# Three graph attention layers over 16 batches: one transpose-and-add moved from TensorE to VectorE blocks and adding transfers

## The reference

```python
def gat(inp, mask, W, a):                      # one attention layer
    h = inp @ W
    e = leaky_relu((h @ a1)[:, :, None] + (h @ a2)[:, None, :], 0.2)
    e = where(mask > 0, e, -9e15)              # layers 2 and 3 only
    return elu(softmax(e, axis=2) @ h)

h = relu(layernorm(x))
out = relu(h @ mlp1_w + mlp1_b)                # 128 -> 256; o1 below
out = elu(gat(out, None, W_fc, a_fc)) + out    # layer 1, 256 wide; z below
out = relu(out @ mlp2_w + mlp2_b)              # 256 -> 128; o2 below
out = elu(gat(out, adj, W_hand, a_hand)) + out # layer 2, 128 wide
x = x + relu(out)
h = relu(layernorm(x))
return x + elu(softmax(masked e) @ (h @ W))    # layer 3, 128 wide
```

## Time and profile before

| | |
|---|---|
| median of three runs | 432.31 us (431.66 to 434.0) |
| span of the profiled execution, first to last instruction | 429.0 us |
| lowest run less that span | 2.7 us |
| median run less that span | 3.3 us |
| granted TensorE clock, mean | 0.994 |
| TensorE busy | 411.1 us (96%) |
| VectorE busy | 357.8 us (83%) |
| ScalarE busy | 315.7 us (74%) |
| GpSimd busy | 24.9 us (6%) |
| DMA traffic | 36.42 MB, mean 85 GB/s |

### The profile page before, as it was taken

One profiled execution on the slowest core, in us unless ns is written; L12 is line 12 of the kernel. 1 busy time (PEld: TensorE's weight loads), 2 busy tenths in 40 slices (PEclk: granted clock), 3 DMA queues, 4 the chain that ended last, 5 costly groups with the idle time before them and its releaser, 6 DMA issues.

```text
span 429.0 us, 8704 instructions
## 1 busy us (share of the span) xinstructions
PE 411.1 (96%) x2544; PEld 352.7 (82%) x2544; DVE 357.8 (83%) x1226; ACT 315.7 (74%) x764; POOL 24.9 (6%) x53
## 2 busy tenths in 40 slices
PE   6999999999999999999999999999999999989782
PEld 4688779887898899797998788989879799869772
DVE  7786588878998898988898868979698899889974
ACT  2655659658796787786878688687867887799774
POOL 0000000000001000010100000100000000000000
PEclk9999999999999999999999999999999999999997
DMA  7854323123423142232222213222320122120001
GB/s 209 278 146 130 105 74 121 74 76 98 125 98 75 53 138 84 52 101 74 75 82 68 75 53 98 79 72 74 80 87 10 49 93 59 45 80 24 27 1 57
DMA packets 39461, 36.42 MB, mean 85 GB/s; under 512 B 4080, under 2 KB 30320, under 8 KB 39408
## 3 DMA queue, kind: packets, MB, share of 16 engines
q1 hardware_dynamic: 37408, 33.17, 26.1%
q10 hardware_dynamic: 2000, 2.63, 1.8%
HBM read 31.46 MB, written 4.32 MB: 83 GB/s over the span
## 4 chain that ended last, share of the span: by engine, by line
PE 87%; DVE 5%; ACT 3%; issue 2%; DMA 1%; SPq 0%; POOL 0%; ACTq 0%; DVEq 0%
PE bank L1530 24%; PE bank L1437 23%; PE bank L1426 13%; PE bank L1416 6%; PE bank L1477 6%; PE bank L1455 6%; PE bank L1445 3%; PE bank L1538 2%; PE bank L1496 1%; PE bank L1466 1%; DMA row<-row_scratch 1%; DVE stats L1036 1%; DVE u L1265 1%; ACT ext L826 1%; ACT e L911 1%
## 5 line engine op out<-in xcount | busy, mean ns | idle before, releaser
L1530 PEld LDWEIGHTS bank<-ext,prob 128*128 128x128 f32 x1024 | 119.6, 192 | 6.3 <-issue 4.9
L1530 PE MATMUL bank<-ext,prob 128*128 128x129 f32 x1024 | 122.1, 275 | 0.3 <-DVE prob L1207 0.2
L1437 PE MATMUL bank<-ext,prob 128*128 128x257 f32 x512 | 119.0, 380 | 0.0
L1437 PEld LDWEIGHTS bank<-ext,prob 128*128 128x128 f32 x512 | 94.8, 190 | 17.3 <-issue 4.5
L1211 DVE SCALAR_TENSOR_TENSOR prob<-prob,square,mask_t 128x512 f32<-128x512 f32 x98 | 70.6, 739 | 0.9 <-ACT prob L859 0.8
L1426 PE MATMUL bank<-wfc_sb,o_t 128*128 128x259 f32 x256 | 64.0, 382 | 0.4 <-ACT o_t L790 0.4
L859 ACT ACTIVATE prob<-row,square 128x512 f32<-128x512 f32 x78 | 54.1, 720 | 0.1
L1426 PEld LDWEIGHTS bank<-wfc_sb,o_t 128*128 128x128 f32 x256 | 46.3, 190 | 9.6 <-issue 4.5
L903 ACT ACTIVATE y<-bank,recip 128x128 f32<-128x128 f32 x128 | 39.3, 369 | 15.3 <-DVE recip L1257 14.2
L911 ACT ACTIVATE e<-y,minus_one 128x512 f32<-128x512 f32 (+1 forms) x70 | 47.7, 688 | 1.4
L1265 DVE SCALAR_TENSOR_TENSOR u<-e,y 128x512 f32<-128x512 f32 (+1 forms) x70 | 44.1, 638 | 4.2 <-issue 2.2
(11 more groups left out here) (98 smaller groups left out, 499.1 us busy)
## 6 DMA issues: line engine op xcount, KB each, us to landing
row<-row_scratch SPq DMA_DIRECT2D x36, 256.0 KB, 3.3
moments_row<-moments_scratch SPq DMA_DIRECT2D x13, 512.0 KB, 3.8
x_in<-in_x SPq DMA_DIRECT2D x16, 256.0 KB, 5.3
x_res<-in_x SPq DMA_DIRECT2D x16, 256.0 KB, 4.6
out<-y_out SPq DMA_DIRECT2D x15, 256.0 KB, 3.9
normed<-in_x_t SPq DMA_DIRECT2D x14, 256.0 KB, 4.3
row_scratch<-square_t SPq DMA_DIRECT2D x144, 0.5 KB
adj_sb<-in_adj ACTq DMA_DIRECT2D x1, 1024.0 KB, 8.1
```

Of the source, the lines that this page charges most:

```text
L1437: last = nc.tensor.matmul(filled[:, 0:H + 1], gat1.targets(b, t, c), gat1.features_and_one(b, t), start=(t == 0), stop=(t == C - 1))
L1530: last = nc.tensor.matmul(filled[:, e * (D + 3):e * (D + 3) + D + 1], L.targets(b, t, c), L.features_and_one(b, t), start=(t == 0), stop=( ...
```

## The change

Step z of batches 2 to 12 (MOVED) takes another way; batches 0, 1 and 13 to 15 keep z_0 and z_1.

- `turnu_0`, `turnu_1` on VectorE turn u in 32x32 blocks into `u_turned` (one buffer). The rest of the transposition, the placing of the blocks, is done by transfers: `move` issues four writes of 128 KB from GpSimd's queue into a scratch in memory (two slots), and `move_in` waits until they have landed and then issues one transfer of 512 KB from the scratch which adds to `o1_t` in place. There is no z_t any more; o1_t has 4 buffers.
- For this the nodes of o1_t stand in another order in the moved batches (`by_blocks`): ScalarE writes o1 so, layer 1's row takes it into account, and mlp2 reads its moving operand in pieces of 32.
- The -1 of elu goes into mlp2's bias, once, for all batches: `sums_w2` (two matmuls with one column and one VectorE instruction).
- `load_again` and `result` go from SyncE's queue to GpSimd's.
- All five strings of ORDER are written anew.

```diff
-O1_DEPTH = 3
+O1_DEPTH = 4
+MOVED = tuple(range(2, 13))
@@ ORDER, sync: no load_again and no result; gpsimd, a line of it
+        max1.0 max1.1 max1.2 load_again.0 load_again.1 max1.3 max2.0 max2.1 move.2 max1.4 load_again.2 move_in.2
...
+        u_turned = sb("u_turned", [P, HT * ROWS, C, 32])
+        blocks_scratch = nc.dram_tensor("blocks_scratch", [2, HT * P * N], fp32, kind="Internal").ap()
-        z_t = sb("z_t", [P, 2, HT, N])
+        def by_blocks(tile):
+            return tile.rearrange("p (a c i) -> p c a i", a=ROWS, c=C)
+            def write_blocks(b):
+                pool.wait_ge(*u_blocks.at(b, 2))
+                if b.n - 2 in MOVED:
+                    pool.wait_ge(*z_moved.two_back(b))
+                places = blocks_scratch[b.slot].rearrange("(f j a n) -> a j f n", f=HT * ROWS, j=32, a=ROWS)
+                for a in range(ROWS):
+                    pool.dma_start(places[a], u_turned[32 * a:32 * (a + 1)].rearrange("p f c i -> p f (c i)")).then_inc(
+                        blocks_written.sem(b), 16)
+            def add_blocks(b):
+                pool.wait_ge(*blocks_written.landed(b))
+                pool.wait_ge(*s1.h_filled.at(b, C))
+                pool.dma_start(o1_t[:, b.of(O1_DEPTH)], blocks_scratch[b.slot].rearrange("(k p n) -> p k n", k=HT, p=P),
+                               accum_op=ALU.add).then_inc(z_moved.sem(b), 16)
...
+            def turn_blocks(b, part):
+                r = slice(part * C // 2, (part + 1) * C // 2)
+                dve.wait_ge(*s1.u.at(b, part + 1))
+                earlier = [n for n in MOVED if n < b.n]
+                if part == 0 and earlier:
+                    dve.wait_ge(*blocks_written.landed(Batch.nth(earlier[-1])))
+                nc.vector.transpose(u_turned[:, :, r].rearrange("p f c i -> p c f i"),
+                                    gat1.u[:, r].rearrange("p c (f i) -> p c f i", i=32)).then_inc(u_blocks.sem, 1)
             def residual1(b, f):
-                nc.vector.scalar_tensor_tensor(out=z_t[:, b.slot, f], in0=bank_of(f"z_{f}", b)[:], scalar=-1.0,
-                                               in1=o1_t[:, b.of(O1_DEPTH), f], op0=ALU.add, op1=ALU.add).then_inc(
-                    z_ready.sem, 1)
+                o1 = o1_t[:, b.of(O1_DEPTH), f]
+                nc.vector.tensor_tensor(o1, bank_of(f"z_{f}", b)[:], o1, ALU.add).then_inc(z_ready.sem, 1)
...
             def mlp2(b):
-                pe.wait_ge(*z_ready.at(b, HT))
+                pe.wait_ge(*(z_moved.landed(b) if moved(b) else z_ready.at(b, HT)))
-                    last = nc.tensor.matmul(filled[:], w2_sb[:, k], z_t[:, b.slot, k],
+                    z = o1_t[:, b.of(O1_DEPTH), k]
+                    last = nc.tensor.matmul(filled[:], w2_sb[:, k], by_blocks(z) if moved(b) else z,
                                             start=(k == 0), stop=(k == HT - 1))
```

More of the change, by code:

```diff
@@ L48 @@
     "sync": """
[L49 to L53, removed]
@@ L66 @@
+        max3.9 result.6 move_in.11 move.12 move_in.12 max2.11 max3.10 max2.12 max2.13 result.9 load_again.12 max1.14
+        result.8 max1.15 max3.11 max3.12 load_again.13 load_again.15 max2.14 result.10 load_again.14 max3.13 max2.15
+        result.11 result.13 max3.14 max3.15 result.12 result.14 guard result.15
     """,
     "scalar": """
-        weights root1.0 root1.1 mlp1_0.0 mlp1_1.0 turn1.1 adjacency root1.2 mlp1_0.1 h1_0.0 mlp1_1.1 turn1.2
-        h1_1.0 root1.3 h1_2.0 h1_3.0 h1_0.1 args1.0 h1_1.1 root1.4 h1_2.1 row1.0 h1_3.1 mlp1_0.2 mlp1_1.2
@@ L621, in factored, with late_transfers, load_x_again, store @@
             return not (general and L.masked)
+        def late_transfers(queue, general):
+            def load_x_again(b):
+                if b.first > 0:
+                    queue.wait_ge(*x1_ready.two_back(b))
+                queue.dma_start(x_res[:, b.slot], x_v[b.n]).then_inc(xres_loaded(b).sem(b), 16)
+            def store(b):
+                rest = slice(0, C)
+                if not general and b.n == B - 1:
+                    queue.wait_ge(*y_ready.at(b, 1))
+                    queue.dma_start(out_v[b.n][:, 0:C // 2], y_out[:, b.slot, 0:C // 2]).then_inc(s_half_stored, 16)
+                    rest = slice(C // 2, C)
+                queue.wait_ge(*y_ready.at(b, 2))
+                queue.dma_start(out_v[b.n][:, rest], y_out[:, b.slot, rest]).then_inc(stored(b).sem(b), 16)
+            return {
+                "load_again": load_x_again,
+                "result": store,
+            }
         def sync_steps(sp, general):
@@ L683, in write_row @@
                     sp.wait_ge(*s.row_loaded.two_back(b))
-                rows = L.scratch[b.slot].rearrange("(c k i) -> k c i", c=C, k=ROWS)
+                order = "(k c i) -> k c i" if L is gat1 and moved(b) else "(c k i) -> k c i"
+                rows = L.scratch[b.slot].rearrange(order, c=C, k=ROWS)
                 for k in range(ROWS):
@@ L713, in sync_steps @@
                 "row0": spread_moments,
-                "load_again": load_x_again,
+                **(late_transfers(sp, general) if general else {}),
                 "row1": lambda b: (write_row(b, gat1), spread_row(b, gat1)),
@@ L744, in pool_steps @@
                 "guard": guard_over_partitions,
+                "move": write_blocks,
+                "move_in": add_blocks,
+                **({} if general else late_transfers(pool, general)),
             }
@@ L1378, in score_columns23, with sums_w2 @@
                                             start=True, stop=True)
+                last.then_inc(s_waf, 1)
+            def sums_w2(b):
+                pe.wait_ge(s_w2, 16)
+                filled = free("sums_w2", b)
+                for k in range(HT):
+                    last = nc.tensor.matmul(filled[:, 0:1], w2_sb[:, k], score_scale[:, 1, 0:1],
+                                            start=(k == 0), stop=(k == HT - 1))
                 last.then_inc(s_waf, 1)
```

394 lines of the change are left out of this document (200 added, 194 removed).

## The result

The changed kernel takes 430.57 us (median of 12 runs, 428.05 to 432.93) against 432.27 (median of 12, 431.26 to 434.0) for the kernel before on the same chip: a ratio of 0.9963, 95% interval 0.9946 to 0.9979. It is faster by 1.6 us (0.9 to 2.3), where 7.9 had been forecast. Its runs also lie further apart than those of the kernel before.

A forecast was written before the change was run, and what follows sets the result against it. TensorE, busy for all 295.00 us from 60 to 355 us, was taken as the bound. Terms -9.6 + 0.4 + 0.5 + 0.8 = -7.9 from 432.3 gave 424.4 us, range 420.5 to 437.5.

The forecast's parts named there:

- the other queues: SyncE, DMA and GpSimd queues in the middle: fewer SyncE issues, more traffic, landings a little longer; cost 0.
- from u to mlp2: New chain of issues and transfers between turnu and mlp2: need 11.9 us, exceeding the time left only in batch 5; +0.5.
- TensorE's side: TensorE loses 88 transposes of z, -9.6 us; sums_w2 adds 0.4; mlp2's reading by pieces costs 0.
- Views: Reading of the profile: TensorE full from 60 to 355 us, so each us of its work there is worth a us.
- the end: Last stores, issued by GpSimd instead of SyncE: second half of result.15 ends later, +0.8 us.
- VectorE's side: VectorE loses 22 additions and gets 22 block transposes at 0.69 us each: no change of its load.
- e: Time of one DMA issue on GpSimd, counted five times per moved batch: taken as 0.87 us.
- W: Landing of a 128 KB block write in memory: taken as 2.7 us.
- A: The 512 KB transfer from memory that adds to o1_t: taken as 4.8 us, bounds 3.8 to 11.4.
- (a): At mlp2 of the batches with least time left: dear GpSimd issues, late adding transfer; slower, 439.2 us; chance 0.21.
- (b): VectorE's scalings and GpSimd's issues get in each other's way: half the gain, 428.2 us; chance 0.20.
- (c): On TensorE, other steps' waits fill the transposes' place, or reading by pieces is slow: 430 to 434 us; chance 0.07.

The follow-up runs named there:

- e12: The kernel before, in its own order, without the 88 transposes of z of batches 2 to 12; 427.8 us, -4.2 against the kernel before.
- e2: The changed kernel without the transfers of move and move_in, mlp2 waiting for the block transposes alone; 425.68 us, -7.5 against the kernel before.
- e4: The changed kernel with the same issues and waits, an eighth of the write bytes and a thirty-second of the adding transfer's; 425.22 us, -7.6 against before.
- e3: The changed kernel with all transfers, the adding one into a spare tile, mlp2 not waiting for the sum; 428.26 us, -4.3 against the kernel before.
- e1: The changed kernel run again, unaltered, beside three variants on one chip; 431.63 us, -1.5 against the kernel before.
- e7: The kernel before with only load_again and result moved to GpSimd's queue; 433.16 us, +0.8 against the kernel before.
- e8: The changed kernel's new order with no batch moved, z back on TensorE, its steps placed; 453.5 us, +20.9 against the kernel before.
- e6: The changed kernel with load_again and result back on SyncE's queue; 430.15 us, -2.7 against the kernel before.
- e5: The changed kernel without the scratch, 16 adding transfers of 32 KB per batch straight into o1_t; 494.75 us, +63.0 against the kernel before.
- e13: The kernel with all transfers but no wait for the sum (e3), without its adding transfer; 424.05 us, -6.6 against the kernel before.

## Why the forecast was wrong

The sign was right, the size was not: -1.6 for -7.9, inside the range. The step that failed is "the other queues", which put what the new traffic does to the transfers that were there before at 0, and it cost 3.2 us. Beside it the term from u to mlp2 was mis-sized, +0.5 for a measured 2.8. TensorE's side came out at -7.5 for -8.4. The three misses, 3.2, 2.3 and 0.9, are the 6.3 us but for rounding. Step by step:

- **Views.** TensorE busy for 295.00 of 295 was read as "each us of TensorE work is worth a us, provided that nothing else comes in its place". e12 refutes it for the order as it was: 9.6 us off, 4.2 gained. The "provided" was the term to work out. VectorE had 252.74 of 295 in the same stretch, in an order of its own, and the maxima and rows form chains of four engines. An engine that is full hides how close the others are behind it. Which of these chains takes the place in e12 was not followed up.
- **TensorE's side, -9.6 + 0.4.** In the new order, with the end's +0.8, that is -8.4; e2 and e4, which have no waits for sums, measured -7.5 and -7.6, with -8.4 inside their intervals. That the number fits is in part luck: the reason given for it, that a us of TensorE's work is worth a us, gives 4.2 for 9.6 in the old order (e12), and what the new order adds, for which the prediction had no term, makes up for most of it. Reading by pieces cost 0, as taken: four records of mlp2 took 1.88 us both in batch 0 (a plain row) and in batch 3 (pieces). Timeline of TensorE, changed kernel:

```profile
47.15 1.88 PE L1532 MATMUL bank<-o_t,w_sb 128*128 128x512 f32 x4
...
102.89 1.88 PE L1532 MATMUL bank<-o_t,w_sb 128*128 128x512 f32 x4
```

- **VectorE's side.** Right: 694 ns a block transpose, VectorE's busy time 358.2 instead of 357.8.
- **From u to mlp2, +0.5: mis-sized.** Measured 2.8 (e3 to e1). e was too dear (0.87, measured 0.61), W too cheap (2.7; the last block write landed 2.7 to 5.5 us after its issue in e1), A too (4.8; measured 6.1 to 7.0 in eight batches, 8.2 to 8.4 in batches 6, 10 and 11), and "the maxima and load_again that stand between fall into W" failed in batch 11, where a maximum of batch 9 still waited for VectorE when the blocks had landed (e1: landed at 301.50, adding transfer issued at 303.31). The windows too were off by up to 5 us (batch 9: 17.8 forecast, 12.7 there). The one batch in which the sum was to come late, 5, has the shortest window (12.2) and got by; mlp2 waited in 4, 6, 7 and 11. Its load was to wait for 1 us or less in total, and waits 4.0 in the changed kernel's trace:

```profile
PEld bank L1532 <- DMA o_t<-blocks_scratch: 4.0, 4, 2.0
```

- **The other queues: the step that failed.** "Landings a little longer, inside A's bounds" looked at the new transfers alone. SyncE's waits for the rows' writes, on which all three layers hang, got 0.37 us longer (1.10 to 1.47). What the traffic does cost 3.2 us (e2 to e3), as much as the waits that I had counted batch by batch. That it does so through the rows is the likely way, not a shown one. The share of the transfers itself was forecast well, 0.42 for 0.45.
- **The end, +0.8.** e7 has +0.8 (-0.0 to +1.6) for the other queue, in the whole kernel. In the trace the last issues take 0.72 to 0.75.
- **Rivals.** (a) named the right place, mlp2 behind a late adding transfer; its issues were not dear and A stayed under the 8.6 from which it decides, in every batch. (b) is refuted in its size: with the 55 issues and few bytes (e4) the time is that of e2, and VectorE's scaling of layer 1 took 549 ns on the mean against 537. The Trainium skill (SBUF — State Buffer, SBUF: two separate sides) has GpSimd locked out in such operations; in e4 that cost nothing measurable. (c) gave the right time, 430 to 434, with a mechanism half right: waits of other steps fill the place, in the old order too (e12). But neither a later mlp2 nor the reading by pieces is behind it, since e2 has both and gains 7.5 us.

Some sums of the prediction are slightly off, and none changes its outcome. Batch 4's steps on VectorE add up to 7.1 us, not 6.9. At an e of 1 us the end costs 1.2, so the time would be 425.4, not 425.1. At a need of 14.5 the loss is 4.1 us, not about 3.

The adding transfer was priced as a read of 3.8 and 1.0 for the target. It takes 6.1 at the least in the changed kernel. The Trainium skill (DMA: Bandwidth & Descriptors, Anatomy of one DMA) fits a transfer on this path as about 2.0 us and its bytes at 436 GB/s, an estimate of 3.2 us for 512 KB. The Trainium skill (Collectives: The Full Stack, The bandwidth ceiling) says of the reduce step of a collective that its add needs two source reads; taken over to this transfer that is 2.0 + 2 x 1.2 = 4.4, an estimate too. The trace is above both.

Left open: why the adding transfer takes 8.2 to 8.4 us in three batches; why the landing of the last block write comes anything from 2.7 to 5.5 us after its issue, with few bytes too (batch 3 of e4: 4.9); through which transfers and steps the traffic costs its 3.2 us; and what fills the place of TensorE's work in e12. A kernel with fewer moved batches was not run, since steps put in by hand cost more than they tell (e8). No kernel that computes the whole result beat the changed kernel by more than its interval; e6 comes nearest.

## What to carry to other kernels

An engine that is busy for 100% of a stretch says where to look, not what its work is worth: take the work away in the order as it stands (e12, one run that leaves a step out and keeps its waits) before building what replaces it, and expect to plan the order anew. Look where a chain of waits begins before reading its shares: in two of the chains shown here the first half or more was missing. And where records of one queue overlap, take busy time over count for a price, not the mean duration (e5). Price a new transfer twice, once for who waits for it and once for the small transfers that it meets: here each cost about 3 us, and only the first was in the sum. A wait of a microsecond in a tightly planned order is not mended by moving the waiting step back; what stands behind it moves too.

## What the runs showed of the hardware

- A transfer of 512 KB from memory that adds to SBUF: 6.1 to 7.0 us from issue to landing, in three batches of eleven 8.2 to 8.4; its issue on GpSimd 1.23 us, against 0.61 for a write of 128 KB and 0.80 for a load of 256 KB. With 16 KB (e4) it still takes 2.7 to 4.5.
- While such a transfer is under way, small writes of another queue land later: SyncE waits 2.18 us for a row's writes instead of 1.09 (e3), which makes 1.47 a row on the mean of all. The Trainium skill (DMA: Bandwidth & Descriptors, SWDGE vs HWDGE vs iDMA) says that the two queues share the same 16 engines, which take turns between their queues; the trace agrees as far as the rows are late with the adding transfer, but plain writes of the same 512 KB (e13) left the rows' mean at 1.09.
- 16 adding transfers of 32 KB from SBUF to SBUF per batch (e5): starts 0.54 us apart, 0.88 us of GpSimd's busy time each, and a maximum behind them lasts until the queue is worked off.
